# Splitting the first two adjacency tiles by halves in a fp32 GNN layer kernel, with an order of its own on VectorE

## The reference

```python
def _layernorm(x, axis=-1, eps=1e-05):
    m = jnp.mean(x, axis=axis, keepdims=True)
    v = jnp.var(x, axis=axis, keepdims=True)
    return (x - m) / jnp.sqrt(v + eps)

h = jnp.maximum(_layernorm(x, axis=-1), 0.0)
agg = jnp.matmul(adj, h)
out = jax.nn.relu(jnp.matmul(agg, W.T) + b)
x = x + out
```

## Time and profile before

| | |
|---|---|
| device time, median of three runs | 384.17 us (383.60 to 384.37) |
| device time of the profiled execution | 383.73 us |
| span in its trace | 381.9 us |
| TensorE matmul busy | 376.7 us, 99% of the span, 1649 instructions |
| VectorE busy | 218.1 us, 57% |
| ScalarE busy | 170.3 us, 45% |
| GpSimd busy | 63.6 us, 17% |
| data moved | 80.25 MB, mean 210 GB/s |

### The profile page before, as it was taken

How to read it: one execution, slowest core, us unless ns; L and a number is a source line. 1 busy time by engine, 2 the same in 40 slices (tenths; PEclk the granted TensorE clock), 3 DMA queues, 4 the chain that set the end, 5 groups by cost and what they waited for, 6 DMA issues and landing times.

```text
span 381.9 us, 4421 instructions
## 1 busy us (share of the span) xinstructions
PE 376.7 (99%) x1649; PEld 308.1 (81%) x1649; DVE 218.1 (57%) x292; ACT 170.3 (45%) x196; POOL 63.6 (17%) x79
## 2 busy tenths in 40 slices
PE   8999999999999999999999999999999999999996
PEld 4788888888888888888888888888888888888885
DVE  4999999995744444444564444444465444444424
ACT  4565556564544343333543333334364334343414
POOL 2787777770010000000001000000000100000000
PEclk9999999999999999999999999999999999999999
DMA  7987787768649565656565856565656675656203
GB/s 239 356 279 264 266 264 257 211 212 322 195 148 349 194 193 193 194 193 203 181 197 189 311 185 197 187 202 185 200 186 206 234 255 187 205 182 205 68 2 110
DMA packets 22774, 80.25 MB, mean 210 GB/s; under 512 B 2464, under 2 KB 2976, under 8 KB 22752
## 3 DMA queue, kind: packets, MB, share of 16 engines
q1 hardware_dynamic: 20736, 72.36, 57.5%
q0 software_dynamic: 2016, 7.60, 5.5%
HBM read 75.76 MB, written 4.19 MB: 209 GB/s over the span
## 4 chain that ended last, share of the span: by engine, by line
PE 96%; DMA 2%; DVE 1%; SPq 1%; ACT 0%; issue 0%
PE bank L370 90%; PE bank L416 6%; DMA x_sb<-x_dram 2%; DVE adj_lo L215 0%; SPq L148 0%; SPq L145 0%; ACT out_sb L346 0%; DVE stats L231 0%; SPq L155 0%; DVE out_sb L284 0%; DVE centred L242 0%; DVE mean_var L236 0%
## 5 line engine op out<-in xcount | busy, mean ns | idle before, releaser
L370 PE MATMUL bank<-adj_hi,h_sb 128*128 128x512 f32 x1024 | 255.0, 390 | 0.0
L215 DVE TENSOR_TENSOR adj_lo<-adj_in,adj_hi 128x1024 fp32r<-128x1024 f32 x127 | 155.4, 1224 | 138.7 <-ACT adj_hi L306 138.7
L370 PEld LDWEIGHTS bank<-adj_hi,h_sb 128*128 128x128 f32 x1024 | 192.2, 188 | 41.0 <-ACT h_sb L317 1.1
L306 ACT ACTIVATE adj_hi<-adj_in 128x1024 fp32r<-128x1024 f32 x127 | 134.5, 1059 | 159.9 <-PE bank L370 157.9
L370 PE MATMUL bank<-adj_lo,h_sb 128*128 128x512 f32 x512 | 137.9, 390 | 0.5 <-DVE adj_lo L215 0.5
L370 PEld LDWEIGHTS bank<-adj_lo,h_sb 128*128 128x128 f32 x512 | 95.9, 188 | 21.3 <-DVE adj_lo L215 1.0
L195 POOL TENSOR_TENSOR rstd<-var_eps,minus_half 128x1 f32<-128x1 f32 x32 | 50.0, 1564 | 2.5
L207 POOL DMA_DIRECT2D out_t_dram<-out_sb x3 | 2.2, 723 | 209.8 <-DVE out_sb L284 209.8
L317 ACT ACTIVATE h_sb<-centred,rstd 128x256 fp32r<-128x256 f32 x32 | 16.3, 508 | 26.7 <-POOL rstd L195 26.6
L231 DVE BATCH_NORM_STATS2 stats<-x_sb 128x6 f32<-128x256 f32 x32 | 13.5, 421 | 4.0 <-DMA x_sb<-x_dram 4.0
L284 DVE TENSOR_TENSOR out_sb<-out_sb,xt_sb 128x512 f32<-128x512 f32 (+1 forms) x17 | 11.1, 659 | 7.6 <-ACT out_sb L346 7.6
(11 more groups left out here) (20 smaller groups left out, 29.0 us busy)
## 6 DMA issues: line engine op xcount, KB each, us to landing
adj_in<-adj_t_dram SPq DMA_DIRECT2D x127, 512.0 KB, 3.7
xt_sb<-x_t_dram POOLq DMA_DIRECT2D x4, 1024.0 KB, 7.3
x_sb<-x_dram SPq DMA_DIRECT2D x7, 512.0 KB, 6.4
out_t_dram<-out_sb POOLq DMA_DIRECT2D x3, 1024.0 KB, 5.0
out_t_dram<-out_sb SPq DMA_DIRECT2D x3, 256.0 KB, 2.0
adj_in<-adj_t_dram SPq DMA_DIRECT2D x2, 256.0 KB, 4.1
x_sb<-x_dram SPq DMA_DIRECT2D x2, 128.0 KB, 3.0
x_sb<-x_dram SPq DMA_DIRECT2D x1, 256.0 KB, 5.8
```

The lines of the kernel that those rows point to most:

```text
L215: nc.vector.tensor_tensor(adj_lo[:, k, :], adj_in[:, k, :], adj_hi[:, k, :].bitcast(fp32), ALU.subtract).then_inc(s_lo, 1)
L306: nc.scalar.activation(adj_hi[:, k, :], adj_in[:, k, :], ACT.Copy).then_inc(s_hi, 1)
L370: last = nc.tensor.matmul(bank(g, kb, c)[:], h_sb[:, t, hp, kb * P:(kb + 1) * P], adj_parts[ap][:, n % U, chunk(c)], start=(t == 0 and (hp ...
```

## The change

The first two adjacency tiles, not the first alone, are loaded in halves of 128x512 (256 KB), each with its own semaphore, rounded in halves on ScalarE, subtracted in halves on VectorE, and summed chunk by chunk on TensorE (`early_tile`). x tiles 2 and 3 come as two transfers of 128 KB, the first in front of adjacency tile 2 and the second between adjacency tiles 2 and 3. VectorE has a written-out order for these tiles: the first half's rest and h rest of tile 1 now come before the moments and the centring of x tile 2, the second half's rest of tile 1 comes between the work on x tiles 2 and 3, and from tile 2 on the loop is as before. The semaphores s_hi and s_lo count chunks for tiles 0 and 1 and whole tiles after that (`made_chunk`, `made_tile`). The diff, cut to its core (renamed waits in `load_adj`, `sum_tile` and the ring's wait on `s_adj` are left out where they only count differently):

```diff
-    X_PIECES = [(0, 1), (1, 2), (2, 4)] + [(t, t + 4) for t in range(4, TILES, 4)]
+    X_PIECES = [(t, t + 1) for t in range(4)] + [(t, t + 4) for t in range(4, TILES, 4)]
...
+        def made_chunk(t, c):
+            return CHUNKS * t + c + 1
+
+        def made_tile(n):
+            return made_chunk(n, CHUNKS - 1) if n < EARLY else CHUNKS * EARLY + n - EARLY + 1
...
-            def load_adj0(c):
-                sp.dma_start(adj_in[:, 0, chunk(c)], adj_v[:, 0, chunk(c)]).then_inc(s_adj0[c], 16)
+            def load_chunk(t, c):
+                sp.dma_start(adj_in[:, t, chunk(c)], adj_v[:, t, chunk(c)]).then_inc(s_early[t][c], 16)
...
             load_x(0)
-            load_adj0(0)
+            load_chunk(0, 0)
             load_x(1)
-            load_adj0(1)
-            load_adj(1)
+            load_chunk(0, 1)
+            load_chunk(1, 0)
+            load_chunk(1, 1)
             load_x(2)
             load_adj(2)
+            load_x(3)
             load_adj(3)
-            load_x(3)
+            load_x(4)
             for n in range(U, GROUPS * TILES):
                 load_adj(n)
-                i = n // 4 + 3
+                i = n // 4 + 4
...
+            def early_rest(t, c):
+                dve.wait_ge(s_hi, made_chunk(t, c))
+                nc.vector.tensor_tensor(adj_lo[:, t, chunk(c)], adj_in[:, t, chunk(c)],
+                                        adj_hi[:, t, chunk(c)].bitcast(fp32), ALU.subtract).then_inc(s_lo, 1)
...
             for t in range(AHEAD):
                 moments(t)
                 centre(t)
-            for t in range(TILES):
-                if t == 0:
-                    first_adj_rest(0)
-                    h_rest(0)
-                    first_adj_rest(1)
-                else:
-                    adj_rest(t)
-                    h_rest(t)
+            early_rest(0, 0)
+            h_rest(0)
+            early_rest(0, 1)
+            early_rest(1, 0)
+            h_rest(1)
+            moments(2)
+            centre(2)
+            early_rest(1, 1)
+            moments(3)
+            centre(3)
+            for t in range(EARLY, TILES):
+                adj_rest(t)
+                h_rest(t)
                 if t + AHEAD < TILES:
                     moments(t + AHEAD)
                     centre(t + AHEAD)
...
+            def early_rounded(t, c):
+                act.wait_ge(s_early[t][c], 16)
+                nc.scalar.activation(adj_hi[:, t, chunk(c)], adj_in[:, t, chunk(c)], ACT.Copy).then_inc(s_hi, 1)
...
-            first_adj_rounded(0)
+            early_rounded(0, 0)
             h_rounded(0)
-            first_adj_rounded(1)
-            for t in range(1, TILES):
+            early_rounded(0, 1)
+            early_rounded(1, 0)
+            h_rounded(1)
+            early_rounded(1, 1)
+            for t in range(EARLY, TILES):
                 adj_rounded(t)
                 h_rounded(t)
...
+            def early_tile(t):
+
+                pe.wait_ge(s_hhi, t + 1)
                 for c in range(CHUNKS):
+                    pe.wait_ge(s_hi, made_chunk(t, c))
+                    add_up(0, t, [c], 0, 0)
+                    pe.wait_ge(s_lo, made_chunk(t, c))
+                    add_up(0, t, [c], 0, 1)
+                    if c == 0:
+                        pe.wait_ge(s_hlo, t + 1)
+                    last = add_up(0, t, [c], 1, 0)
                 last.then_inc(s_pe, 1)
...
-            first_tile()
-            for t in range(1, TILES):
+            for t in range(EARLY):
+                early_tile(t)
+            for t in range(EARLY, TILES):
                 sum_tile(0, t, range(CHUNKS), False).then_inc(s_pe, 1)
```

More of the change, by code:

```diff
@@ L37, in bass_preln_gnn_residual @@
     WARM_UP = 11
+    EARLY = 2
     SPLIT_AT = 4
     OUT_AT = 8
-    X_PIECES = [(0, 1), (1, 2), (2, 4)] + [(t, t + 4) for t in range(4, TILES, 4)]
+    X_PIECES = [(t, t + 1) for t in range(4)] + [(t, t + 4) for t in range(4, TILES, 4)]
     x_v = x.rearrange("(p t) d -> p t d", t=TILES)
@@ L85, in bass_preln_gnn_residual @@
         s_adj = [sem(f"adj_landed{k}") for k in range(U)]
-        s_adj0 = [sem(f"first_adj_landed{c}") for c in range(CHUNKS)]
+        s_early = [[sem(f"adj{t}_chunk{c}_landed") for c in range(CHUNKS)] for t in range(EARLY)]
         s_xt = sem("xt_landed")
@@ L99, in bass_preln_gnn_residual @@
         s_hi = sem("adj_hi_made")
-        s_hi0 = sem("first_adj_hi_chunk_made")
         s_lo = sem("adj_lo_made")
-        s_lo0 = sem("first_adj_lo_chunk_made")
         s_pe = sem("tiles_summed")
@@ L152, in load_adj @@
                 if n >= U:
-                    sp.wait_ge(s_hi, n - U + 1)
-                    sp.wait_ge(s_lo, n - U + 1)
+                    sp.wait_ge(s_hi, made_tile(n - U))
+                    sp.wait_ge(s_lo, made_tile(n - U))
                 sp.dma_start(adj_in[:, n % U, :], adj_v[:, t, g * GW:(g + 1) * GW]).then_inc(s_adj[n % U], 16)
             load_x(0)
-            load_adj0(0)
+            load_chunk(0, 0)
             load_x(1)
-            load_adj0(1)
-            load_adj(1)
+            load_chunk(0, 1)
+            load_chunk(1, 0)
+            load_chunk(1, 1)
             load_x(2)
             load_adj(2)
+            load_x(3)
             load_adj(3)
-            load_x(3)
+            load_x(4)
             for n in range(U, GROUPS * TILES):
                 load_adj(n)
-                i = n // 4 + 3
+                i = n // 4 + 4
                 if n % 4 == 0 and i < len(X_PIECES):
@@ L213, in adj_rest @@
                 k = n % U
-                dve.wait_ge(s_hi, n + 1)
+                dve.wait_ge(s_hi, made_tile(n))
                 nc.vector.tensor_tensor(adj_lo[:, k, :], adj_in[:, k, :], adj_hi[:, k, :].bitcast(fp32),
                                         ALU.subtract).then_inc(s_lo, 1)
-            def first_adj_rest(c):
-                if c < CHUNKS - 1:
-                    dve.wait_ge(s_hi0, c + 1)
-                else:
[L223 to L226, removed]
+            def early_rest(t, c):
+                dve.wait_ge(s_hi, made_chunk(t, c))
+                nc.vector.tensor_tensor(adj_lo[:, t, chunk(c)], adj_in[:, t, chunk(c)],
+                                        adj_hi[:, t, chunk(c)].bitcast(fp32), ALU.subtract).then_inc(s_lo, 1)
             def moments(t):
@@ L299, in adj_rounded @@
             def adj_rounded(n):
-                g, t = divmod(n, TILES)
                 k = n % U
-                act.wait_ge(s_adj[k], 16 * (n // U + (k > 0)))
+                act.wait_ge(s_adj[k], 16 * (n // U + (k >= EARLY)))
                 if n >= U:
@@ L374, in add_up @@
                 return last
-            def first_tile():
-                pe.wait_ge(s_hhi, 1)
+            def early_tile(t):
+                pe.wait_ge(s_hhi, t + 1)
                 for c in range(CHUNKS):
[L380 to L391, removed]
+                    pe.wait_ge(s_hi, made_chunk(t, c))
[5 more added lines that the diff above has]
+                    last = add_up(0, t, [c], 1, 0)
                 last.then_inc(s_pe, 1)
@@ L400, in sum_tile @@
                                 pe.wait_ge(s_hhi, n + 1)
-                            pe.wait_ge(s_hi, n + 1)
+                            pe.wait_ge(s_hi, made_tile(n))
                         elif ap == 1:
-                            pe.wait_ge(s_lo, n + 1)
+                            pe.wait_ge(s_lo, made_tile(n))
                         elif g == 0:
```

## The result

The changed kernel takes 382.92 us in the median of eight runs (382.67 to 383.08), the kernel before 384.08 us in its eight (383.48 to 384.52): a ratio of 0.9971, 95% interval 0.9962 to 0.998. That is 1.16 us less where 0.77 was forecast against the median and 0.80 by the steps; by the interval the gain is 0.8 to 1.5 us. In the profiled executions it is 383.73 to 382.79 us, and the spans are 381.9 and 381.0.

The account below looks back on a forecast made before the run. TensorE bounds the kernel, so only its early idle stretches can give time: 0.70 us of stall plus 0.1 of slower restart make 0.80, taken off the median of 384.17 for 383.4 us; range 382.9 to 384.3.

Parts of the forecast that it names:

- What bounds the kernel: Whole kernel: TensorE is busy 376.7 of 381.9 us, so time can only come from its idle stretches near the start.
- The stall and its cause: TensorE before 11.20 us: 0.70 us of waiting for tile 1's low part, late through VectorE's order behind x tiles 2 and 3.
- The transfers: Early loads: same bytes and queue, tile 1 in two issues; two bounds, tile 1's halves landing at 7.22 and 7.97 or 7.54 and 8.61.
- the low bound: Early loads: a half takes 0.75 us; halves at 7.22 and 7.97, x 2 at 8.45, tile 2 at 10.09, x 3 at 10.57.
- ScalarE, VectorE, GpSimd: Tiles 1 and 2: h 1 from about 7.75, VectorE's first half at 8.01, second at 10.01; tile 2's power takes 1.12 us.
- who waits: GpSimd's power at 9.99 beside VectorE's half rest at 10.01: VectorE wins; rival, VectorE held off, 0.2 us lost, chance 0.02.
- TensorE: Start of the stream: tile 1 runs through at 0.232 us a matmul, tile 2 starts at 12.35 instead of 13.15, gain 0.80 us.
- the rival with more than the gain: TensorE's start: a faster pace before 14.07 and smaller tile 0 stalls, gain 0.95 to 1.1 us, 383.1 us; chance 0.10.
- The sum: Whole kernel: profiled 383.73 becomes 382.93 us; median 384.17, 0.44 above, less the gain gives 383.4 us, 0.2% less.
- the line of 0.2%: Whole kernel: a measurement tells a change of about 0.2%, 0.77 us, from none; the expected gain lies on it.
- x tile 3 as the new wait: VectorE's moments 3: a landing at 13.1 costs TensorE 2.05 us against a gain of 0.80, 385.4 us; chance 0.08.
- The rival that gives part of the gain back: Tile 2's low part late by the high bound: gain 0.55, 383.6 us; with late x tiles 4 to 7, 0.25, 383.9; chance 0.22.

Follow-up runs that it names:

- order_alone: The kernel before, with VectorE doing moments and centring of x tile 2 behind the whole rest and h rest of tile 1: 384.21 us, ratio 1.0007.
- old_order: The changed kernel with VectorE's old order (x tile 2's moments and centring ahead of both halves of tile 1): 383.83 us, ratio 1.0006.
- tile1_load_whole: The changed kernel with adjacency tile 1 loaded in one 512 KB transfer, rounding and rests still by halves: 383.44 us, ratio 0.999.
- the second comparison: The changed kernel once more, unedited, beside the kernel before: 382.77 us in five runs against 384.16 in twelve, ratio 0.9968.
- x3_late: The changed kernel with the transfer of x tile 3 issued behind adjacency tile 3: 383.78 us, ratio 0.9998.
- x3_later: The changed kernel with x tile 3 issued behind the piece with x tiles 4 to 7: 386.73 us, ratio 1.0065.
- high_first_centre_later: The changed kernel with tile 0's high-by-high pass first on TensorE, and VectorE's rest of tile 2 before x tile 3's centring: 382.60 us, ratio 0.9961.
- pe_high_first: The changed kernel with TensorE doing the high-by-high pass of both halves of tile 0 before the low passes: 382.88 us, ratio 0.9967.

## Why the prediction was right

**What bounds the kernel** held: all that was gained was gained ahead of 12.3 us, and the rest of TensorE's stream has the length it had.

**The stall and its cause** held, and more tightly than put: it is the landing of x tiles 2 and 3 plus 2.28 us, in three profiles; order_alone and old_order show that neither the new order nor the halves win time by themselves. What the step left out is a second wait, h 1 on ScalarE behind a whole adjacency tile, which the first profile hides and the second shows (0.45 us).

**The transfers**: the low bound was taken, and right for tile 2 in the changed kernel's profile (10.07 for 10.09), while the first half of tile 1 at 7.34 and x tile 2 near 8.6 lie between the bounds (7.22 and 7.54, 8.45 and 9.09). In other executions the landings of the same issues differ by a microsecond and more (tile 1 whole: 7.96, 8.37, 8.38, 9.06), so that it fitted here is in part luck. The forecast treated landings as fixed and counted the halved transfer of tile 1 as no gain of its own; tile1_load_whole shows that without it some 0.6 to 0.9 us of the gain in the median go, with intervals that only just part (0.9981 begins the one and ends the other).

**ScalarE, VectorE, GpSimd**: each start within 0.01 us on VectorE, the power within 0.01; on ScalarE h 1 came 0.13 later than forecast (7.88 for 7.75), which cost nothing. On who waits, the row at 10.00 is again ahead of the half rest at 10.01, which keeps its 0.68 us while the power is drawn out to 1.11. So by the recorded starts the later one, VectorE, wins. "Issue order, not op shape, decides who blocks", says the Trainium skill, "SBUF — State Buffer", section "Who interferes with whom"; the trace does not agree, as far as starts 0.01 us apart can tell which of the two came first.

**TensorE**: tile 2 at 12.22 for 12.35. Of the 0.13, 0.07 is an earlier first product (6.03 against 6.10), which scatters between executions (6.01 to 6.33 in the three profiles of the kernel before) and so is luck, and the rest the pace: from 9.05 on starts are 0.227 apart, not 0.232, as the rival with more than the gain had it. What sets the pace stays open.

**The sum** was too small. Two terms were mis-sized. The stall taken away was 0.80 us by the first profile's landings and 0.93 in the trace of after. And the 0.44 us by which the median lay above the profiled execution was carried over unchanged: in the eight runs it was 0.35 before and is 0.13 after (382.92 less 382.79), so the scatter shrank with the stall. Together that makes the 1.16 of the medians (1.39 in the second comparison). The measured 382.92 lies 0.02 us inside the lower end of the range, 382.9, and that it lies inside at all is luck: the forecast was 383.4. The measured ratio, 0.2% to 0.38% under one, lies at and beyond the line of 0.2% on which the forecast sat, and the likelier of the two outcomes by the forecast was no difference (0.48), with faster at 0.44.

**The rivals**: the slower one, x tile 3 as the new wait, has its mechanism confirmed by x3_late and x3_later to the hundredth (2.28 us from landing to restart, against 2.23 + 0.05), but in the changed kernel that tile is in time: issued at 4.50 it was there at 10.4, before 10.62. Its price was too low, 2.05 us for a landing at 13.1 where x3_later lost 3.8 to 4.0 with one at 12.96, since the half clock after the stall was not in it. The rival that gives part of the gain back had its landings too late for both profiles of after, and the piece with x tiles 4 to 7, feared at 14.05, was issued at 5.46 and landed 7.5 us later, near 13.0, where VectorE wanted it at 13.15.

## What to carry to other kernels

Where the start of a kernel is a race between transfers and a bound engine, ask of every wait in an in-order engine's list what stands behind it that is already possible; move that ahead, and split it so that the chain behind the wait isn't made late in turn. Order alone and halves alone were each worth nothing that could be measured here (at most 0.1 and 0.3 us by their intervals), together 1.2 to 1.4 us. One part was never run by itself, TensorE's going through tile 1 chunk by chunk; by the rows of after, pass by pass would want the second half's low part at 9.51 + 4 x 0.227 = 10.42, and it was done at 10.69, so an estimated 0.3 us hang on it. And read landings as ranges: take two or three profiles, of long executions too, before you call one stall the cause, and count the spread of the runs as something that a change may take away.

## What was not expected of the hardware

An idle stretch of TensorE of 1.93 us in the middle of dense work was followed by the granted clock at 0.50 from 15.8 to 19.2 us, which cost 1.7 us beyond the stall itself; in old_order stalls of 1.57 and 0.27 us had the same after them (0.50 from about 13.6 to 17.0 us). In both the clock was still at 1.00 during the stall and fell after TensorE had restarted, at 15.24 and 11.49, and while it was busy. It did not happen every time: one of the five runs of x3_later kept a mean clock of 0.999. After stalls of 0.2 to 1.0 us in the other profiles the clock stayed at 1.00. The Trainium skill, "TensorE: Matmul & The Clock Gate", section "HAM oscillation — how this bites in real kernels", tells of waits for data between bursts of matmuls that take the clock down again and again. These two traces agree that a wait for data can do it, but here it fell once in each, and after shorter waits (1.93 us, and 1.57 with 0.27, where the page's are of about 3 to 5 us).

The landing of a transfer that is issued at the same time and in the same order varies by more than a microsecond between executions: x tile 2, issued at 3.5 us, took 5.1 us in the changed kernel's profile and 4.9 in its second, 4.4 in high_first_centre_later, 5.6 in pe_high_first and 6.2 in old_order, and in all five the issues up to it are the same.
